# Half of the attention transposes moved from TensorE to VectorE, as nine 32x32 blocks a step, in a decoder kernel

## The chip, the core and the metric

The kernel runs on one core of a Trainium2 chip. A core has four engines that compute, each with its own instruction queue: TensorE (PE in the profile, with its weight loads as PEld), VectorE (DVE), ScalarE (ACT) and GpSimd (POOL); SyncE (SP) issues transfers. Semaphores order the queues against each other. The metric is the time of the whole kernel on the device in microseconds.

## What is computed

A decoder of four layers on x of 16 sequences x 128 positions x 256 channels. The change lies in layer 2, whose first part is grouped-query attention with 16 heads of 128 channels over 4 key/value heads, with a mask that leaves each query a window of 32 positions and the first 4:

```python
def _sink_window_mask(t):
    pos = jnp.arange(t)
    q = pos[:, None]
    k = pos[None, :]
    return (k <= q) & ((k < SINK) | (k >= q - WINDOW + 1))      # SINK 4, WINDOW 32

def _masked_softmax(scores, mask):
    floor = jnp.finfo(scores.dtype).min
    ms = jnp.where(mask, scores, floor)
    row_max = jnp.max(ms, axis=-1, keepdims=True)
    ...
    ex = jnp.exp(ms - row_max) * mask.astype(scores.dtype)
    denom = jnp.maximum(jnp.sum(ex, axis=-1, keepdims=True), 1e-09)
    return ex / denom
```

The other parts of layer 2 are a cross attention in which each query keeps its 54 largest scores, and a feed-forward part with activations and weights rounded to 8-bit levels. Each part ends with a residual sum and a layer norm.

## The kernel before

All ten parts of the decoder stand one after the other. Only layer 2 is touched: `layer2_all` (L2538) weaves its three parts into one software pipeline over the 16 sequences. `STEPS` is 23; step i (i from 0 to 22) does the self-attention of sequence i, the end of it and the start of the cross attention of i-1, the selection of i-2, the end of the cross attention of i-3, the rounding for the feed-forward part of i-4, the upper product and the inner rounding of i-5, the lower product of i-6 and the last norm of i-7. Each engine has its own `step(i)` (ScalarE L2776, VectorE L3022, TensorE L3231), a list of calls in a hand-written order. Each call waits for the semaphores that it needs and holds up what is queued behind it on its engine.

The self-attention of one sequence: queries and keys are projected (`project_kv`, `project_q` in four quarters q, L3077, copied out by `queries_out`), `scores` (L3089) puts 8 heads (a half h) into two PSUM banks, `shift` adds the mask and takes the row maxima on VectorE, `exps` runs on ScalarE, and `normalise` (L2867) divides on VectorE. For the product with the values the probabilities must stand with the keys on the partitions. So `turn_probs` (L3097) transposes the 8 heads of a half on TensorE, each a 128x128 f32 transpose, into the half's banks; `probs_moved` (L2686) copies them on ScalarE to `probsT`; `attend` (L3107) multiplies.

What stands around the change, in program order:

- VectorE, step i: copy of the values (L3027), `shift` for both halves, `largest(i-2)`, `normalise(i, 0)`, `scale_up(i-5)` (L2941), `select(i-2)` (L2898, ends with L2906 to L2910), `normalise(i, 1)` (L2870 to L2874), `add(i-1)` (L2876; L2878 is the residual sum, L2884 the variance), `scale_inner(i-5)` (ends with L2951), `freshen(i-1)`, `scale_x(i-4)` (ends with L2937), `scale_down(i-6)` (L2953; L2955 raises back_made), `add_x(i-3)`, `finish(i-7)`, and in the first 12 steps a piece of the rounding of the weights.
- TensorE, step i: both `scores`, `scores_x(i-2)`, `project_kv(i+1)`, `turn_probs_x(i-3)`, `up(i-5)`, `turn_inner(i-6)`, `output(i-1)`, `read_x(i-3)`, `project_q(i+1, 0)`, `down(i-6)`, `project_q(i+1, 1)`, `turn_probs(i, 0)`, `output_x(i-3)` (L3145; it waits for "added", the end of `add(i-1)`), `project_q(i+1, 2)` and `(i+1, 3)`, `turn_probs(i, 1)`, `turn_x(i-1)`, `turn_xq(i-4)`, `attend(i, 0)`, `queries_x(i-1)` (L3166), `attend(i, 1)`. `project_q(.., 3)` waits until `queries_out(.., 1)` has emptied the bank.
- ScalarE, second half of step i: `queries_out(i+1, 0)`, `root_x(i-1)` (L2726, waits for the variance of `add`), `root_n`, `root_f`, `queries_out(i+1, 1)`, `probs_moved(i, 0)`, `inner_rounded(i-5)` (L2756, waits for L2951), `queries_out(i+1, 2)`, `xq_rounded(i-4)` (L2738, waits for L2937), `queries_out(i+1, 3)`, `probs_moved(i, 1)`, `x_out(i-1)` (L2720), and so on.

`turn_probs(i, 1)` writes into banks 2 and 3. Bank 3 also holds the lower product of the feed-forward part, so from step 6 on it waits for "back_made" of `scale_down(i-6)`, which is on VectorE in the same step.

## Time and profile before

| | us |
|---|---|
| median of 3 runs | 2474.65 (2472.78 to 2476.43) |
| the profiled execution, and its span | 2477.81, 2476.0 |
| granted TensorE clock over the span, share of full | 0.928 |
| busy: TensorE, VectorE, ScalarE, GpSimd | 2114.1, 1859.2, 1482.2, 198.2 |
| layer 2 in the span | about 1521 to 2103 |

The profile gives for each instruction its line in the kernel, its start and duration, and, in square brackets, how long its engine idled before it and which instruction ended that wait. A matmul's weight load (LDWEIGHTS) is a record of its own on PEld and overlaps with the multiply before it; the starts of loads show the pace of TensorE's queue. Within a queue, records of neighbours overlap by some tens of nanoseconds. Step i of the layer is counted from VectorE's copy L3027: step 0 at 1525.32, step 9 at 1795.01.

### The profile page before, as it was taken

What the parts mean: (1) busy time and instruction counts of PE and PEld (TensorE: products, weight loads), DVE (VectorE), ACT (ScalarE), POOL (GpSimd) and SP (SyncE); (2) the same over time, 40 slices, a digit from 0 to 9 for tenths busy, and PEclk for the clock granted to TensorE, in tenths of its full rate; (3) what the DMA queues carried; (4) which work ended last, traced back from release to release, by engine and by line L of the source; (5) the groups of instructions that cost most, each with busy time, mean ns of one, the idle gap of its engine ahead of it and who ended that gap; (6) DMA issues with size and microseconds to landing.
All of it is one profiled execution on the core that took longest, in us unless ns stands there. A gap on an engine that the chain in (4) does not pass through costs nothing. (4 is left out here: it accounts for less than half of the span.)

```text
span 2476.0 us, 42560 instructions
## 1 busy us (share of the span) xinstructions
PE 2114.1 (85%) x17048; PEld 1606.8 (65%) x17048; DVE 1859.2 (75%) x3345; ACT 1482.2 (60%) x2484; POOL 198.2 (8%) x148
## 2 busy tenths in 40 slices
PE   7996458999999999999863798999999974888755
PEld 4665336777777787777751456888888862555633
DVE  4777666888998888898769525567887766678687
ACT  3654255777777767777546423667777765455346
POOL 0000100110100011010100240000000000100301
PEclk8999678999999999999986899999999996999977
DMA  3000012122222222222232464111010000200001
GB/s 155 2 2 12 13 55 73 52 65 54 66 54 61 71 80 63 55 66 55 60 112 94 146 150 152 59 22 45 27 33 5 6 16 1 79 1 1 15 1 34
DMA packets 162482, 130.96 MB, mean 53 GB/s; under 512 B 118256, under 2 KB 145520, under 8 KB 155632
## 3 DMA queue, kind: packets, MB, share of 16 engines
q1 hardware_dynamic: 158448, 121.83, 16.1%
q0 software_dynamic: 3840, 6.43, 1.3%
q8 instruction: 136, 2.23, 0.4%
q14 instruction: 58, 0.48, 0.1%
HBM read 106.42 MB, written 21.79 MB: 52 GB/s over the span
## 5 line engine op out<-in xcount | busy, mean ns | idle before, releaser
L1587 DVE SCALAR_TENSOR_TENSOR ctx_chan<-l1a_raw,l1a_cw,ctx_chan 128x1024 f32<-128x1024 f32 x192 | 231.9, 1276 | 3.5 <-issue 3.5
L1195 PE MATMUL banks<-x_chan,l1a_wp 128*128 128x512 f32 x512 | 224.4, 596 | 3.6 <-ACT l1a_vt L1483 3.6
L1195 PEld LDWEIGHTS banks<-x_chan,l1a_wp 128*128 128x128 f32 x512 | 97.6, 191 | 121.0 <-issue 116.3
L3086 PE MATMUL banks<-x_chan,more_weights_ahead 128*128 128x128 f32 x1024 | 121.9, 276 | 1.2 <-ACT l2a_kT L2670 1.2
L3086 PEld LDWEIGHTS banks<-x_chan,more_weights_ahead 128*128 128x128 f32 x1024 | 118.6, 192 | 4.3 <-ACT l2a_kT L2670 2.0
L1232 PE MATMUL banks<-l1a_wo,l1a_oT 128*128 128x256 f32 x512 | 118.4, 385 | 0.0
L3122 PE MATMUL banks<-l2a_wo,l2a_oT 128*128 128x256 f32 x512 | 114.3, 381 | 0.0
L1203 PE MATMUL banks<-l1a_wz,x_chan 128*128 128x256 f32 x512 | 114.1, 381 | 0.0
L1182 POOL TENSOR_TENSOR l1a_al<-l1a_aT,l1a_outer 128x1024 f32<-128x1024 f32 x32 | 74.9, 2362 | 481.3 <-DVE l1a_aT L1647 481.3
L1232 PEld LDWEIGHTS banks<-l1a_wo,l1a_oT 128*128 128x128 f32 x512 | 97.0, 192 | 13.8
L3122 PEld LDWEIGHTS banks<-l2a_wo,l2a_oT 128*128 128x128 f32 x512 | 96.2, 190 | 14.7 <-issue 1.5
L1203 PEld LDWEIGHTS banks<-l1a_wz,x_chan 128*128 128x128 f32 x512 | 97.0, 192 | 13.1 <-issue 0.5
L2683 ACT ACTIVATE l2a_masked<-l2a_masked,l2a_rowmax 128x128 f32<-128x128 f32 x256 | 98.9, 392 | 8.1 <-DVE l2a_rowmax L2865 6.5
L1431 ACT ACTIVATE l1a_raw<-banks 128x1024 f32<-128x1024 f32 x64 | 65.5, 1023 | 48.1 <-PE banks L1195 48.1
L2678 ACT ACTIVATE l2a_qT<-banks 128x512 f32<-128x512 f32 x64 | 37.9, 594 | 66.6 <-PE banks L3086 66.6
L123 PE MATMUL banks<-ident,x_tok 128*128 128x128 f32 x224 | 42.9, 356 | 40.7 <-ACT x_tok L191 18.0
L3644 ACT ACTIVATE l3a_probsT<-banks 128x512 f32<-128x512 f32 x64 | 38.1, 596 | 59.3 <-PE banks L3810 59.3
L1461 ACT ACTIVATE l1a_oT<-l1a_go 128x1024 f32<-128x1024 f32 x32 | 33.9, 1058 | 66.2 <-DVE l1a_go L1712 66.2
L1642 DVE TENSOR_TENSOR_SCAN l1a_e<-ctx_tok 128x1024 f32<-128x1024 f32 x32 | 71.4, 2273 | 1.1 <-DMA ctx_tok<-l1a_rows_mem 1.1
L1772 DVE TENSOR_TENSOR l1a_vt<-banks,l1a_vt 64x512 f32<-64x512 f32 x64 | 44.4, 694 | 36.1 <-PE banks L1260 36.0
L1433 ACT ACTIVATE ctx_chan<-banks,l1a_cw 128x1024 f32<-128x1024 f32 x64 | 71.0, 1109 | 0.0
L3027 DVE COPY l2a_vals<-l2a_ready 128x512 f32<-128x512 f32 x16 | 6.8, 427 | 81.9 <-PE banks L3112 72.0
(648 smaller groups left out, 5706.8 us busy)
## 6 DMA issues: line engine op xcount, KB each, us to landing
l1a_sq<-l1a_norm_mem SPq DMA_DIRECT2D x16, 1024.0 KB, 4.7
ctx_tok<-l1a_rows_mem SPq DMA_DIRECT2D x16, 1024.0 KB, 8.0
ctx_chan<-in_ctxT_dram SPq DMA_DIRECT2D x3, 2048.0 KB, 18.1
l1f_wgu<-in_l1f_wgu_dram SPq DMA_DIRECT2D x4, 1408.0 KB, 11.5
moe_sums<-l1x_zero SPq DMA_DIRECT2D x2, 2176.0 KB, 16.4
l1a_wp<-in_l1a_wp_dram SPq DMA_DIRECT2D x8, 512.0 KB, 5.7
l1f_wgu<-moe_sums SPq DMA_DIRECT2D x8, 512.0 KB, 7.4
x_chan<-in_xT_dram SPq DMA_DIRECT2D x4, 512.0 KB, 5.5
```

The source lines that it names most:

```text
L1182: P.tensor_tensor(heads(al, h), heads(aT, h), bc(outer[:], 1, HALF), ALU.mult).then_inc(s["al_made"], 1)
L1195: mm = MM(projected(i, u)[:, q * 512:(q + 1) * 512], wp[:, c, u * 128:(u + 1) * 128], g.xT[:, c, t0:t0 + 512], start=c == 0, stop=c == 1)
L1203: mm = MM(unit(2 + h)[:, b * 256:(b + 1) * 256], g.xT[:, c, t0:t0 + S], wz[:, c, :], start=c == 0, stop=c == 1)
L1232: mm = MM(unit(h)[:, b * 256:(b + 1) * 256], oT[:, HALF * h + 2 * b + r, :], wo[:, r, :], start=r == 0, stop=r == 1)
L1431: A(raw[:, u, :, CONV - 1:], now, ACT.Copy)
L1433: A(conv[:, u, :], projected(i, u), ACT.Copy, scale=cw[:, c, CONV - 1:]).then_inc(s["tap"], 1)
L1587: V.scalar_tensor_tensor(t, raw[:, u, :, j:j + S], cw[:, c, j:j + 1], t, ALU.mult, ALU.add).then_inc(s["conv_done" if step == 2 else "conv ...
L1642: V.tensor_tensor_scan(heads(e, h).rearrange("p k n -> p (k n)"), rows[:, h * 1024:(h + 1) * 1024], floor, 0.0, ALU.add, ALU.max).then_inc ...
L1772: V.tensor_tensor(highs(vt, q), quarter(q)[64:128], highs(vt, q), ALU.add).then_inc(s["vr_made"], 1)
L2683: ins = A(probs[:, k, :], masked[:, k, :], ACT.Exp, bias=rowmax[:, k:k + 1], scale=128 ** -0.5, accum_out=rsum[:, k:k + 1])
L3086: mm = mm_(ps[:, 4 + q % 2, k * 128:(k + 1) * 128], wq[:, c, SHARE * q + k, :], g.xT[:, c, tile(i)], start=c == 0, stop=c == 1)
L3122: mm = mm_(ps[:, 6, 0:D], oT[:, h, :], wo[:, h, :], start=h == 0, stop=h == HEADS - 1)
```

## The change

Half 0 of the heads is no longer transposed on TensorE. The new `turn_first` on VectorE transposes it in 32x32 blocks, from `probs` straight to `probsT`. Of the 16 blocks of a head only nine can hold anything but zero under the mask; the list `WINDOWED` names them as (block of queries, block of keys), and the others are set to zero once by a memset at the start. Each of the nine instructions takes its block for all 8 heads of the half: 32 partitions, 8 x 32 elements each. `turn_first(i)` stands on VectorE between `select(i-2)` and `normalise(i, 1)`. TensorE's `turn_probs(i, 0)` and ScalarE's `probs_moved(i, 0)` are gone, and `attend(i, 0)` waits for the new semaphore. The remaining `turn_probs(i)` keeps its place behind `project_q(i+1, 3)` and now has both waits on the banks.

```diff
@@ layer2_all
+        WINDOWED = ((0, 0), (1, 0), (1, 1), (2, 0), (2, 1), (2, 2), (3, 0), (3, 2), (3, 3))
...
-            def probs_moved(i, h):
-                act.wait_ge(s["probs_turned"], i * 2 + (h + 1))
-                A(heads(probsT, h), half_banks(h), ACT.Copy).then_inc(s["probs_out"], 1)
+            def probs_moved(i):
+                act.wait_ge(s["probs_turned"], i + 1)
+                A(heads(probsT, 1), half_banks(1), ACT.Copy).then_inc(s["probs_out"], 1)
@@ step(i), ScalarE
                 if more:
                     queries_out(i + 1, 1)
-                if now:
-                    probs_moved(i, 0)
                 if on(i - 5):
                     inner_rounded(i - 5)
...
                 if now:
-                    probs_moved(i, 1)
+                    probs_moved(i)
@@ VectorE
+            def turn_first(i):
+                v.wait_ge(s["normed"], i * 2 + 1)
+                for a, b in WINDOWED:
+                    queries, keys = slice(32 * a, 32 * a + 32), slice(32 * b, 32 * b + 32)
+                    ins = V.transpose(heads(probsT, 0)[keys, :, queries], heads(probs, 0)[queries, :, keys])
+                ins.then_inc(s["first_turned"], 1)
@@ step(i), VectorE
                 if on(i - 2):
                     select(i - 2)
                 if i < B:
+                    turn_first(i)
                     normalise(i, 1)
...
+            V.memset(heads(probsT, 0), 0.0).then_inc(s["cleared"], 1)
             v.wait_ge(s["loaded"], 16)
+            v.wait_ge(s["cleared"], 1)
@@ TensorE
-            def turn_probs(i, h):
-                pe.wait_ge(s["normed"], i * 2 + (h + 1))
-                if h == 0 and i >= 5:
+            def turn_probs(i):
+                pe.wait_ge(s["normed"], i * 2 + 2)
+                if i >= 5:
                     pe.wait_ge(s["gu_done"], i - 4)
-                if h == 1 and i >= 6:
+                if i >= 6:
                     pe.wait_ge(s["back_made"], i - 5)
                 for k in range(HALF_HEADS):
-                    mm = turn(half_banks(h)[:, k, :], heads(probs, h)[:, k, :], g.ident[:])
+                    mm = turn(half_banks(1)[:, k, :], heads(probs, 1)[:, k, :], g.ident[:])
                 mm.then_inc(s["probs_turned"], 1)
             def attend(i, h):
                 pe.wait_ge(s["vals_moved"], i + 1)
-                pe.wait_ge(s["probs_out"], i * 2 + (h + 1))
+                pe.wait_ge(s["probs_out" if h else "first_turned"], i + 1)
@@ step(i), TensorE
                 if more:
                     project_q(i + 1, 1)
-                if now:
-                    turn_probs(i, 0)
                 if on(i - 3):
                     output_x(i - 3)
                 if more:
                     project_q(i + 1, 2)
                     project_q(i + 1, 3)
                 if now:
-                    turn_probs(i, 1)
+                    turn_probs(i)
```

## Rows read from the trace of the kernel before

**Rows 1.** Steps 6 to 13: stretch, length; busy us of PE, PEld, DVE, ACT, POOL; clock, DMA.

```profile
1698.28:1956.23 257.95, 257.95 (x1722) 217.76 (x1721) 201.95 (x531) 192.09 (x512) 4.29 (x8) 1.00 0.08 23
```

**Rows 2.** Timeline of VectorE in step 9: start, us, engine, line, instruction, [idle before].

```profile
1810.80 0.29 DVE L2910 TENSOR_SCALAR l2a_px<-l2a_px,l2a_sumx 128x128 f32<-128x128 f32 x1
1811.00 0.16 DVE L2870 TENSOR_SCALAR l2a_rsum<-l2a_rsum 128x8 f32<-128x8 f32 x1
...
1812.58 0.42 DVE L2878 TENSOR_TENSOR x_tok<-banks,x_tok 128x256 f32<-128x256 f32 x1
...
1818.14 0.48 DVE L2955 SCALAR_TENSOR_TENSOR ctx_tok<-banks,l2a_sh,l2f_row 128x256 f32<-128x256 f32 x1
...
1827.25 0.43 DVE L3027 COPY l2a_vals<-l2a_ready 128x512 f32<-128x512 f32 x1 [3.00 <-PE banks L3112]
```

**Rows 3.** Timeline of TensorE's weight loads in step 9.

```profile
1816.05 0.91 PEld L3104 LDWEIGHTS banks<-ident,l2a_masked 128*128 128x128 f32 x8
1816.92 0.73 PEld L3153 LDWEIGHTS banks<-l2a_wox,l2a_ox 128*128 128x128 f32 x4
...
1821.36 0.91 PEld L3104 LDWEIGHTS banks<-ident,l2a_masked 128*128 128x128 f32 x8
```

**Rows 4.** Groups by line and shape in layer 2: count, busy us, mean ns, idle before.

```profile
L3027 DVE COPY l2a_vals<-l2a_ready 128x512 f32<-128x512 f32 x16 | 6.8, 427 | 81.9 <-PE banks L3112 72.0 <-ACT l2a_ready L2674 9.9
L2688 ACT ACTIVATE l2a_probsT<-banks 128x1024 f32<-128x1024 f32 x32 | 32.7, 1023 | 10.1 <-PE banks L3104 10.0
```

**Rows 5.** Timeline of VectorE at the end of the kernel, instructions without waits between.

```profile
2468.98 0.74 DVE L144 BATCH_NORM_STATS2 ln_stats_buf<-x_tok 128x6 f32<-128x256 f32 x2
...
2470.69 1.38 DVE L3531 TENSOR_SCALAR x_tok<-x_tok,ln_moments_buf,ln_rstd_buf 128x256 f32<-128x256 f32 x4
```

**Rows 6.** Timeline of VectorE and of the weight loads, step 0.

```profile
1544.51 0.17 DVE L2870 TENSOR_SCALAR l2a_rsum<-l2a_rsum 128x8 f32<-128x8 f32 x1 [2.37 <-ACT l2a_masked L2683]
...
1544.95 1.23 DVE L2874 TENSOR_TENSOR l2a_masked<-l2a_masked,l2a_rsum 128x1024 f32<-128x1024 f32 x1
...
1548.99 0.91 PEld L3104 LDWEIGHTS banks<-ident,l2a_masked 128*128 128x128 f32 x8
```

**Rows 7.** Timeline of ScalarE and of the weight loads, step 2.

```profile
1598.32 0.20 ACT L2728 ACTIVATE ln_rstd_buf<-ln_rstd_buf 128x1 f32<-128x1 f32 x1 [0.48 <-DVE ln_rstd_buf L2884]
...
1599.03 0.60 ACT L2678 ACTIVATE l2a_qT<-banks 128x512 f32<-128x512 f32 x1 [0.51 <-PE banks L3086]
...
1599.59 3.65 PEld L3086 LDWEIGHTS banks<-x_chan,more_weights_ahead 128*128 128x128 f32 x32
```

**Rows 8.** Timeline of VectorE and of the weight loads, step 3.

```profile
1624.88 0.42 DVE L2878 TENSOR_TENSOR x_tok<-banks,x_tok 128x256 f32<-128x256 f32 x1
...
1628.02 0.73 PEld L3153 LDWEIGHTS banks<-l2a_wox,l2a_ox 128*128 128x128 f32 x4
```

**Rows 9.** Timeline of VectorE, the weight loads and ScalarE, step 5.

```profile
1685.21 0.42 DVE L2878 TENSOR_TENSOR x_tok<-banks,x_tok 128x256 f32<-128x256 f32 x1
...
1687.95 0.73 PEld L3153 LDWEIGHTS banks<-l2a_wox,l2a_ox 128*128 128x128 f32 x4
...
1688.44 0.16 DVE L2951 RECIPROCAL l2a_rh<-l2a_sh 128x1 f32<-128x1 f32 x1
...
1689.18 0.96 ACT L2758 ACTIVATE ctx_tok<-ctx_tok,l2a_toround,l2a_rh 128x704 f32<-128x704 f32 x1
...
1693.57 1.02 ACT L2688 ACTIVATE l2a_probsT<-banks 128x1024 f32<-128x1024 f32 x1 [0.28 <-PE banks L3104]
```

**Rows 10.** Timeline of VectorE and of the weight loads, step 6.

```profile
1721.64 0.48 DVE L2955 SCALAR_TENSOR_TENSOR ctx_tok<-banks,l2a_sh,l2f_row 128x256 f32<-128x256 f32 x1
...
1724.63 0.91 PEld L3104 LDWEIGHTS banks<-ident,l2a_masked 128*128 128x128 f32 x8
```

**Rows 11.** Timeline of VectorE and of the weight loads, step 15.

```profile
2011.60 0.48 DVE L2955 SCALAR_TENSOR_TENSOR ctx_tok<-banks,l2a_sh,l2f_row 128x256 f32<-128x256 f32 x1
...
2012.19 1.57 PEld L3104 LDWEIGHTS banks<-ident,l2a_masked 128*128 128x128 f32 x8 [4.89 <-issue]
```

More of the change, by code:

```diff
@@ L2584, in layer2_all @@
         s = L.sem_set("loaded w_loaded next_loaded wox_loaded staged queries keys values q_out k_out v_out vals_moved scores maxed "
-                      "masked lowered exped rs normed probs_turned probs_out pv o_out out added "
+                      "masked lowered exped rs normed cleared first_turned probs_turned probs_out pv o_out out added "
                       "wr_loaded w_summed w_floored w_scaled w_spread wt_loaded w_rows w_divided w_rounded w_quantised "
```

## The prediction

> **What bounds the kernel now.** I read the windows of the layer first. In the eight steps 6 to 13 TensorE is busy for 257.95 of 257.95 us at full clock, VectorE for 201.95 and ScalarE for 192.09 [rows 1]. So TensorE sets the step of 32.24 us, in which VectorE works 25.2 and ScalarE 24.0, and the step repeats itself up to step 14. Next I read VectorE's own order in step 9: it idles 3.0 us at the seam of two steps, waiting for the last attention product (L3112), then works with almost no gap [rows 2]. So on a busy-time account this change takes work from the full engine and gives it to one that has room. The views that decide are others: where in the step the added work stands, and how long before its use TensorE gets what VectorE makes behind that place. I measure such a lead as TensorE's weight load (it starts the group) minus the end of the VectorE instruction it waits for, minus the 0.11 us from such an end to the load: in step 15, where the load did wait, 2012.19 against 2011.60 + 0.48 [rows 11].
>
> In step 9 the two leads are:
> - output_x (L3153) waits for add (L2878): 1816.92 against 1812.58 + 0.42 + 0.11 = 1813.11, lead 3.81 us [rows 2, 3].
> - the second turn_probs (L3104) waits for scale_down (L2955, "back_made"): 1821.36 against 1818.14 + 0.48 + 0.11 = 1818.73, lead 2.63 us [rows 2, 3]. This is the tighter one, and it exists only from step 6 on. Steps 7 to 14 show the same pair at the same distances.
>
> **What goes.** The eight TensorE transposes of half 0: the loads of L3104 start at 1816.05 and those of L3153 behind them at 1816.92, so the group takes 0.87 us of TensorE's queue [rows 3]. That is the whole possible gain: 16 x 0.87 = 13.9 us. The copy of half 0 out of the banks (L2688, 1.02 us, one of two a step) leaves ScalarE [rows 4], which idles 8 us a step; by itself that gains nothing. attend(i, 0) waits for the block transposes instead; in step 9 they are done at about 1814.2, and it stands behind the second turn_probs, at 1821.36 or later.
>
> **What comes.** Nine VectorE instructions a step, each on 32 partitions with 8 x 32 = 256 elements per partition, in a row without waits between them. The trace has no block transpose and no 32-partition instruction. The nearest rows are f32 instructions of 256 elements per partition. Alone one takes 0.42 us [rows 2]. Back to back they overlap: four take 1.38 us, (1.38 - 0.42) / 3 = 0.32 us from start to start; two take 0.74 [rows 5]. I bound the nine from 9 x 0.32 = 2.9 us (full overlap) to 9 x 0.42 = 3.8 us (none) and take 9 x 0.345 = **3.1 us**, near the lower end, since instructions that do not wait for each other show the overlap. Call it T.
>
> The page "VectorE: DVE Perf Modes" of the Trainium skill (section on the three transpose paths) gives 311 ns for a VectorE transpose of 128x128 bf16. The 128-element TENSOR_SCALAR just ahead of the new place takes 0.29 us [rows 2]. An estimate from the page: 0.02 us more each than a plain instruction, T = 3.1 to 3.2, the sum at most 1.4 us higher.
>
> The memset of 1024 elements costs at most about a plain instruction of that size, 1.2 us [rows 6], and stands in the 9.9 us that VectorE idles before its first copy [rows 4]: nothing. If that cover were gone it would be 1.2 us once.
>
> **Where T falls.** It stands between select (ends with L2910) and normalise(i, 1) (starts with L2870). In step 9 L2910 ends at 1811.09 and L2870 starts at 1811.00 [rows 2]: there is no idle to fill, and none up to L2955. Everything behind comes T later: normalise 1, add, scale_inner, freshen, scale_x, scale_down. The 3 us of idle lie at the seam, behind all of them, so they can't shield them. Now step by step, with the change of each step's length:
>
> - Steps 0 and 1: no select yet. VectorE idles 2.37 us for the exponentials just where T stands, so only 3.1 - 2.37 = 0.7 us come through; normalise ends at 1544.95 + 1.23 = 1546.18, its use is at 1548.99 [rows 6]. TensorE keeps its gain: -0.87 each, **-1.7**.
> - Step 2: select is there, T comes through whole. ScalarE's root_x (L2728, at 1598.32) waits for add's variance, and queries_out(1), 0.60 us, stands behind it. root_x moves to 1601.42, queries_out(1) starts 0.1 us before its 0.20 are over, at 1601.52, and ends 1602.12; project_q(3), which needs it, starts near 1602.2. It started in the middle of the 3.65 us of loads from 1599.59, at 1601.38 [rows 7]. **+0.85**, that is T - 2.25.
> - Steps 3 and 4: output_x waits for add. 1625.30 + 0.11 + 3.1 = 1628.51 against 1628.02 [rows 8]: **+0.5** each, T - 2.6.
> - Step 5: add ends at 1685.63; + 0.11 + 3.1 = 1688.84 against 1687.95: +0.9. Here inner_rounded is on ScalarE for the first time. It starts at 1689.18 and waits for VectorE's L2951, which moves to 1688.60 + 3.1 = 1691.7 [rows 9]. Behind it stand queries_out(2), xq_rounded and queries_out(3), with it an estimated 3.2 us, so probs_moved starts near 1694.9, where TensorE's shift of 0.9 alone would bring it to 1694.5. x_out, and with it queries_x, is late by the difference. **+1.4**.
> - Step 6: scale_down ends at 1722.12, the load starts at 1724.63 [rows 10]: lead 2.40, **+0.7**.
> - Steps 7 to 14: output_x may start at 1813.11 + 3.1 = 1816.21, 0.71 us early. project_q(2) and (3) follow, and turn_probs could load at 1820.65, but scale_down lets it only at 1818.73 + 3.1 = 1821.83, against 1821.36 before. The gain is gone in a wait of 1.2 us: 8 x (3.1 - 2.63) = **+3.8**. ScalarE reached probs_moved 9.3 us after add's old end in step 5; here that is 1822.3, and the transposes come out only at about 1823.0, so it adds nothing.
> - Step 15: no projections are left, and TensorE already waits 4.89 us (loads) at turn_probs for L2955 [rows 11]. T goes in whole: **+3.1**. The transposes behind that wait run at the lower clock (eight loads in 1.57 us against 0.91) [rows 3, 11]; they do so already, so I add nothing.
> - Steps 16 to 22 have no transposes.
>
> Sum: -1.7 + 0.85 + 1.0 + 1.4 + 0.7 + 3.8 + 3.1 = **+9.2 us**. The profiled execution took 2477.81 us (span 2476.0), 3.2 above the median of 2474.65; the difference is put on the median: 2483.8. About 14 us per us of T: with T = 2.9 the sum is +6.4, with 3.8 it is +19.0.
>
> The next thing that would be late, were back_made's wait not there, is VectorE's own round: of 3.0 us at the seam 3.0 - 2.63 = 0.4 stay, whatever T is, because TensorE is pushed back with it.
>
> **Rivals.**
> - *The blocks are cheap, and the kernel is faster.* The plain copy of 512 elements takes 0.43 us [rows 4], half the time per element. If the transposes ran at that rate, 256 elements would take 0.29 us alone, 0.20 from start to start, T = 1.8. Then -1.7 in steps 0 and 1, -0.45 in 2, -1.6 in 3 and 4, -0.4 in 5, -0.6 in 6, 8 x -0.83 = -6.6, +1.8 in 15: **-9.6 us, 2465**. From T = 3.1 - 9.2 / 14 = 2.44 down the kernel is faster. Against it: the 256-element instructions of rows 5 don't show it. The page "Vector Engine (DVE) Microarchitecture Reference" (3.8) says the transposing front-end sustains one element per cycle per lane; that is a rule against this rival, and no row here tests it.
> - *Nothing measurable.* If T is 2.5 to 2.75 (a 32-partition instruction with a shorter start), or one lead is longer than it looks because the waits order themselves anew, the 0.87 and the wait balance: **+1 to +4 us, 2478**. For it: the gap between gain and loss is only 0.5 us a step. Against it: no pair of rows 5 is closer than 0.32 us.
> - *The blocks are dear.* Four-byte elements could take twice the cycles, or each block be one instruction with its own start. Nine at about 0.6 us (0.27 more than 0.33) are T = 5.4: 9.2 + 14 x 2.3 = **+41 us, 2516**. For it: nothing in the trace excludes it. Against it: f32 costs no more per element than that in any row here.
> - *The gain holds.* VectorE would have to take T out of its idle time. It can't: the idle is behind the instructions that TensorE waits for [rows 2]. It is part of the first rival's chance.
>
> **How the numbers follow.** Forecast (T 2.9 to 3.8, +6.4 to +19.0, so 2481 to 2494) 0.64; dear 0.14; nothing measurable 0.13; cheap 0.09. The predicted time is 2484. The range of 2477 to 2497 holds the forecast and most of the rival beside it, and the lower edge of the dear one, about 0.8. A measurement of this kernel can tell about 0.2%, 5 us, from no change. Slower by more than that: nearly all of the forecast and the dear case, 0.76; within it: the case of nothing measurable and a little of its neighbours, 0.14; faster: the cheap case and a T just above it, 0.10.
>
> **What would show it.** In the profile after: nine transposes a step with 0.32 to 0.42 us from start to start between L2910 and L2870; a step from 7 to 14 of 32.24 + (T - 2.63) = 32.7 us; TensorE with a wait of about 1.2 us at turn_probs, ended by VectorE's scale_down, and one of some 0.2 us before output_x; VectorE's idle at the seam down from 3.0 to about 0.4; in step 15 a wait of over 7 us. Steps 0 and 1 should be shorter by 0.9. A step under 32.24 us would make the forecast wrong through T; a wait that ends on something other than scale_down would make it wrong in its mechanism.

## The result and the profile after

The changed kernel takes **2497.60 us** (median of 4 runs, 2492.26 to 2500.84) against 2473.74 for the kernel before (4 runs, 2472.78 to 2476.43): ratio 1.0092, 95% interval 1.0075 to 1.0109. It is slower by 23.9 us; 9.2 were forecast, and the time lies 0.6 us above the upper end of the range. The profiled execution took 2498.36 us (span 2496.6, clock 0.928). TensorE's busy time fell from 2114.1 to 2098.9 us, ScalarE's from 1482.2 to 1465.8, VectorE's rose from 1859.2 to 1923.0. Everything that was to be unloaded is unloaded, and the kernel is slower.

The line numbers shift: L3033 is the copy of the values (L3027 before), L2884 the residual sum of `add` (L2878), L2961 the instruction of "back_made" (L2955), L3113 `turn_probs` (L3104), L3162 `output_x` (L3153), L2879 the new block transposes.

First the windows of steps 6 to 13, which answer [rows 1] (columns as there), then the group of the new instructions (count, busy us, mean ns, idle before):

```profile
1701.74:1970.90 269.16, 254.01 (x1651) 211.67 (x1658) 233.41 (x603) 183.98 (x504) 4.29 (x8) 1.00 0.07 22
```

```profile
L2879 DVE STREAM_TRANSPOSE l2a_probsT<-l2a_masked 32x256 f32<-32x256 f32 x144 | 62.6, 435 | 1.8
```

Eight steps take 269.16 us, 33.64 each, where they took 257.95. TensorE was busy all of that time before; now it has 15 us of gaps. Neither queue is full: VectorE works 233.4 of 269.2 us. So the step is set by waits that run back and forth between the two. The timeline of VectorE in step 9 answers [rows 2] (start, us, engine, line, instruction):

```profile
1802.67 0.43 DVE L3033 COPY l2a_vals<-l2a_ready 128x512 f32<-128x512 f32 x1 [0.52 <-PE banks L3121]
...
1818.46 0.29 DVE L2916 TENSOR_SCALAR l2a_px<-l2a_px,l2a_sumx 128x128 f32<-128x128 f32 x1
1818.66 4.02 DVE L2879 STREAM_TRANSPOSE l2a_probsT<-l2a_masked 32x256 f32<-32x256 f32 x9
1822.71 0.17 DVE L2869 TENSOR_SCALAR l2a_rsum<-l2a_rsum 128x8 f32<-128x8 f32 x1
...
1824.30 0.42 DVE L2884 TENSOR_TENSOR x_tok<-banks,x_tok 128x256 f32<-128x256 f32 x1
...
1829.87 0.48 DVE L2961 SCALAR_TENSOR_TENSOR ctx_tok<-banks,l2a_sh,l2f_row 128x256 f32<-128x256 f32 x1
```

The nine take 4.02 us (4.02 or 4.03 in every step; T is 4.03 below), and the next instruction starts 4.05 us after their start. One lasts 0.435 us (the group's mean above). From start to start that is (4.02 - 0.435) / 8 = 0.448 us, more than one lasts: they do not overlap at all. Everything behind them is late by about T. Seen from the copy, L2884 starts at 21.63 us, where it was 17.57, and L2961 at 27.20, where it was 23.13; the idle before the next copy (the seam of two steps) fell from 3.00 to 0.31 us. Whom that hits stands in TensorE's own timeline of the same step, which answers [rows 3]:

```profile
1824.87 1.10 PE L3162 MATMUL banks<-l2a_wox,l2a_ox 128*128 128x256 f32 x4 [0.89 <-DVE x_tok L2884]
...
1830.50 1.06 PE L3113 MATMUL banks<-ident,l2a_masked 128*128 128x128 f32 x8 [0.96 <-DVE ctx_tok L2961]
```

Both waits of the prediction are there, ended by the two instructions that it named. PE's idle counts from the modelled end of the matmul before, so it comes out shorter than the delay. The prediction measured by the starts of the weight loads, and these give the delay:

```profile
1824.84 0.73 PEld L3162 LDWEIGHTS banks<-l2a_wox,l2a_ox 128*128 128x128 f32 x4 [1.05 <-issue]
1825.59 3.76 PEld L3095 LDWEIGHTS banks<-x_chan,more_weights_ahead 128*128 128x128 f32 x32
1830.47 0.85 PEld L3113 LDWEIGHTS banks<-ident,l2a_masked 128*128 128x128 f32 x8 [1.12 <-issue]
```

The loads of output_x start 22.17 us after the copy; in the kernel without the blocks (below), where nothing waits, they start at 21.04. That is a delay of 1.13 us. The transposes start 4.88 us behind the loads of `project_q` (1830.47 - 1825.59), without a wait 3.67: a delay of 1.21 us. Together they are 2.34 us, near 0.87 + 1.40, the gain used up and the growth of the step.

Three places at the beginning and the end of the pipeline follow. Step 5: the timelines of TensorE and of ScalarE, then the windows of TensorE's wait and of the work behind it (columns as in [rows 1]; the third number from the end is the granted clock):

```profile
1689.80 1.75 PE L3162 MATMUL banks<-l2a_wox,l2a_ox 128*128 128x256 f32 x4 [2.49 <-DVE x_tok L2884]
```

```profile
1692.66 0.97 ACT L2759 ACTIVATE ctx_tok<-ctx_tok,l2a_toround,l2a_rh 128x704 f32<-128x704 f32 x1 [1.33 <-DVE l2a_rh L2957]
```

```profile
1687.30:1689.70 2.40, 0.01 (x1) 0.00 (x0) 2.27 (x6) 0.00 (x0) 0.00 (x0) 1.00 0.00 0
1689.80:1692.00 2.20, 2.20 (x8) 1.89 (x9) 2.10 (x5) 0.78 (x3) 0.00 (x0) 0.57 0.00 0
1692.00:1695.80 3.80, 3.80 (x29) 3.80 (x29) 3.45 (x14) 2.73 (x4) 0.00 (x0) 0.80 0.00 0
```

After 2.49 us without work TensorE's granted clock, full until then, is 0.57 and 0.80 in the two stretches behind: it was at the lower of its two levels, 1.2 GHz, for part of them. The 32 loads of `project_q` take 5.01 us there instead of the 3.76 of step 9. Behind the waits of 2.35 us in step 2 and 2.09 us in step 3 the clock stayed at 1.00. And step 15, which answers [rows 11]:

```profile
2026.68 2.04 PE L3162 MATMUL banks<-l2a_wox,l2a_ox 128*128 128x256 f32 x4 [6.42 <-DVE x_tok L2884]
...
2032.30 1.94 PE L3113 MATMUL banks<-ident,l2a_masked 128*128 128x128 f32 x8 [3.58 <-DVE ctx_tok L2961]
```

**Where the 23.9 us come from.** The steps are taken from one copy of the values to the next, the changed kernel's minus those of the kernel before. Steps 0 and 1: -0.57 and -0.87 us. Step 2: +1.75. Steps 3 and 4: +1.46 and +1.44. Step 5: +3.49. Step 6: +1.41. Steps 7 to 14: 8 x 1.40 = +11.2. Together +19.3. In step 15 L2961 starts 27.18 us after the copy against 23.13, +4.05, and from the copy of step 15 to the first matmul of the next layer the profile after takes 4.3 us more, this delay included. That makes 23.6 us, the measured difference within its interval. In this one profile layer 2 also began 3.27 us earlier than in that of before, though nothing ahead of it was changed, so the two profiled executions differ by 20.55 us only.

### The profile page after: what moved, and what is told of

It is laid out like the page before. It is cut to its first block and busy times, and to the rows that moved or that the text cites. A ratio compares the mean times of both kernels' runs of the same rounds, so it can differ in the third digit from the quotient of the medians.

```text
span 2496.6 us, 42374 instructions
## 1 busy us (share of the span) xinstructions
PE 2098.9 (84%) x16871; PEld 1593.0 (64%) x16920; DVE 1923.0 (77%) x3490; ACT 1465.8 (59%) x2468; POOL 196.4 (8%) x148
## 5 line engine op out<-in xcount | busy, mean ns | idle before, releaser
L123 PEld LDWEIGHTS banks<-ident,x_tok 128*128 128x128 f32 x224 | 34.9, 188 | 48.3 <-ACT x_tok L191 19.6
L1260 PE MATMUL banks<-l1a_uw,l1a_al 64*64 64x128 f32 x512 | 65.2, 280 | 0.0
```

The source lines that it names most:

```text
L123: mm = nc.tensor.transpose(g.ps[:, n % 2, t * 128:(t + 1) * 128], g.x[:, t0 + t, c * 128:(c + 1) * 128], g.ident[:])
```

## Experiments

Ratios are against the kernel before, run on the same chip at the same time; the brackets hold the 95% interval. T is the time that the added instructions take on VectorE, read from the trace. Where blocks are left out or replaced, that half of the heads comes out wrong; such a kernel is for its time alone.

### How much of the loss hangs on T: none, four, six of the nine

```diff
-                    turn_first(i)
...
-                pe.wait_ge(s["probs_out" if h else "first_turned"], i + 1)
+                if h:
+                    pe.wait_ge(s["probs_out"], i + 1)
+                else:
+                    pe.wait_ge(s["normed"], 2 * i + 1)
```

> The changed kernel without its nine block transposes: half 0 of the heads is transposed by nobody, so the attention output of those heads is left out of what is computed rightly; all else stands as in the changed kernel. Theory A (only the time T that the transposes put ahead of add and scale_down on VectorE costs; TensorE's 0.87 us a step is a real gain while nothing is late): T = 0, all leads hold, 15 steps shorter by 0.87 us, 13 us less than the kernel before, ratio 0.9947; steps 7 to 14 take 31.37 us. Theory B (another wait takes over once TensorE is shorter, ScalarE's order or a bank wait, and part of the 24 us lost is that): less than 6 us gained, steps near 32 us, with a TensorE wait that ends on ScalarE.

```diff
-                for a, b in WINDOWED:
+                for a, b in WINDOWED[:4]:
```

> The changed kernel with the first four of the nine blocks only; the other five are left out. Theory A: from the trace after, a transpose costs 0.448 us from start to start, T = 1.8 us. That is under both leads even with TensorE 0.87 us ahead (2.63 - 0.87 = 1.76 at turn_probs, to 0.03 us), so steps 7 to 14 take 31.4 us; step 2 gains 0.5, steps 3 and 4 0.8 each, step 15 loses 1.8. Sum about -10 us against the kernel before, ratio 0.996. Theory B (a cost of mixing the transposes in at all, a switch of VectorE's mode or a port, beside their own durations): no better than the kernel before.

With `WINDOWED[:6]`:

> The changed kernel with the first six of the nine blocks; the other three are left out. Theory A (the step pays for what T exceeds the lead of 2.63 us by): 6 x 0.448 = 2.7 us, steps 7 to 14 take 32.24 + 0.05 = 32.3 us, the step of the kernel before. Steps 0 and 1 gain 1.7, step 15 loses 2.7, steps 2 to 6 lose about 1.4 in all. Sum +3 us, ratio 1.001 (0.999 to 1.003). Theory B (the loss grows with VectorE's busy time from the first block on, without a threshold): two thirds of the changed kernel's +24, or 4 blocks' -5 plus 0.4 of the way: +6 to +16, ratio 1.0025 to 1.0065.

Measured: none 0.9960 (0.9944 to 0.9975), steps of 31.37 us; four 0.9978 (0.9967 to 0.9989), steps of 31.38; six 1.0011 (1.0001 to 1.0021), steps of 32.27. The steps are as expected in all three. The whole of none and of four gained less than their expectations (0.9947 and 0.996; the latter lies outside the interval); the table at the end of this part says where that went. The window 1740 to 1960 of none, the group of the four and, of the six, the transposes and the wait that they cause in step 9:

```profile
1740.00:1960.00 220.00, 219.63 (x1448) 184.84 (x1454) 176.70 (x466) 162.14 (x442) 3.76 (x7) 1.00 0.05 16
```

```profile
1803.72 1.77 DVE L2879 STREAM_TRANSPOSE l2a_probsT<-l2a_masked 32x256 f32<-32x256 f32 x4
```

```profile
1807.34 2.66 DVE L2879 STREAM_TRANSPOSE l2a_probsT<-l2a_masked 32x256 f32<-32x256 f32 x6
```

```profile
1817.80 1.06 PE L3113 MATMUL banks<-ident,l2a_masked 128*128 128x128 f32 x8 [0.71 <-DVE ctx_tok L2961]
```

Without the blocks TensorE is full again, and its step is 32.24 - 0.87 = 31.37: in the steps the gain of the prediction is real and of its size. With four, six and nine blocks the step is 29.61 us + T: 31.38 at 1.77, 32.27 at 2.66, 33.64 at 4.03. TensorE's own 31.37 is the floor, reached at T = 1.76, and at T = 2.63 the step equals the 32.24 of before. That is the lead that the prediction read from [rows 2, 3] and put against T; 0.87 of it pays for TensorE's gain.

### The transposes added to the kernel before, nothing taken away

```diff
@@ step(i), VectorE, kernel before
                 if i < B:
+                    turn_first(i)
                     normalise(i, 1)
```

> The kernel before, complete, and the nine block transposes beside it at the same place of VectorE, into the same tile; TensorE's transposes and ScalarE's copy stay and overwrite it (the copy waits for the blocks too, which are done 2 us earlier). Theory A: what TensorE saves is worth nothing from step 2 on, because VectorE's scale_down and add set it; steps 6 to 14 take 33.64 us as in the changed kernel, steps 0 and 1 stay as before; 1 to 3 us slower than the changed kernel, some 26 us over the kernel before, ratio 1.010 to 1.011. Theory B (part of the loss comes from taking work out of TensorE's and ScalarE's order): clearly faster than the changed kernel. Theory C (TensorE's time adds up with the wait): slower than the changed kernel by 0.87 x 14 = 12 us, ratio 1.015.

Measured: 1.0109 (1.0090 to 1.0129), steps 7 to 14 of 33.62 to 33.65 us. TensorE in step 9:

```profile
1828.10 1.06 PE L3115 MATMUL banks<-ident,l2a_masked 128*128 128x128 f32 x8 [0.95 <-DVE ctx_tok L2965]
```

The step is the same 33.64 us whether TensorE and ScalarE keep their share or not. With the share kept, the wait before output_x is gone (TensorE arrives 0.87 us later) and the one of 0.95 us at turn_probs remains. So the loss is VectorE's addition alone, and what TensorE saves in these steps is spent in waiting. Theory C, that TensorE's time adds up with the wait, falls. The early steps add a control for the clock: in step 5 TensorE waits 1.61 us there, the clock stays at 1.00, the 32 loads take 3.76 us, and the step grows by 2.17 us (30.64 to 32.81) instead of 3.49.

### The same nine, behind the instruction that TensorE waits for

```diff
-                    turn_first(i)
                     normalise(i, 1)
...
@@ scale_down(j), behind the instruction of back_made
+                if j + 6 < B:
+                    turn_first(j + 6)
@@ step(i), VectorE
                 if on(i - 6):
                     scale_down(i - 6)
+                elif i < B:
+                    turn_first(i)
```

> The changed kernel, complete, with all nine block transposes moved on VectorE from between select and normalise to just behind the first instruction of scale_down (in steps 0 to 5: behind scale_x). Theory A: VectorE does the same work, but only attend(i, 0) waits for it. In steps 7 to 14 they end at 23.61 + 4.03 + 0.11 = 27.75 us into the step, attend loaded at 27.61 before: +0.14 us a step. Steps 1 to 4 gain 0.8 to 0.9 each, step 0 loses 0.5, step 5 1.4, step 6 0.4, step 15 1.7. Sum about +2 us against the kernel before, ratio 1.0006 (0.998 to 1.003), some 22 us faster than the changed kernel. Theory B (VectorE as a whole is too full with 64 us more work): as slow as the changed kernel, ratio 1.009.

Measured: 1.0005 (0.9992 to 1.0019), steps 6 to 14 of 31.7 to 32.6 us. Step 9, VectorE and TensorE:

```profile
1812.40 4.02 DVE L2879 STREAM_TRANSPOSE l2a_probsT<-l2a_masked 32x256 f32<-32x256 f32 x9
```

```profile
1816.56 1.96 PE L3124 MATMUL banks<-l2a_probsT,l2a_vals 128*128 128x512 f32 x4 [0.76 <-DVE l2a_probsT L2879]
```

The same 4.02 us on the same engine, and the loss is gone: it came from the place of the work, not from its amount. Now `attend(i, 0)` waits for them, for 0.76 us, so the gain is not there either.

### Why the nine take 4.02 us

First the block transposes replaced by plain copies of the same slices, at the same place:

```diff
-                    ins = V.transpose(heads(probsT, 0)[keys, :, queries], heads(probs, 0)[queries, :, keys])
+                    ins = V.tensor_copy(heads(probsT, 0)[keys, :, queries], heads(probs, 0)[queries, :, keys])
```

> The changed kernel with nine plain copies of the same 32-partition, 8 x 32 element slices in place of the nine transposes, across the same quarters of the partitions; the blocks land unturned, so the output of those heads is not what is to be computed. It asks what makes a transpose cost 0.448 us from start to start. Theory C (it is the transposing itself: plain instructions overlap and copies move two f32 a cycle): 0.20 us from start to start, T = 1.8, steps 7 to 14 take 31.4 us, ratio 0.996 to 0.998 as with four blocks. Theory D (32-partition slices or the way across quarters cost it): about 0.45, T = 4.0, ratio 1.009.

```profile
L2879 DVE COPY l2a_probsT<-l2a_masked 32x256 f32<-32x256 f32 x144 | 40.9, 284 | 1.8
```

```profile
1808.85 2.66 DVE L2879 COPY l2a_probsT<-l2a_masked 32x256 f32<-32x256 f32 x9
```

Ratio 1.0012 (1.0002 to 1.0022), steps of 32.27 us, just as with six transposes of the same 2.66 us: only T counts. But from start to start the copies are (2.66 - 0.284) / 8 = 0.297 us apart, where neither theory had them: shorter than transposes, yet again without any overlap. So it is not the transposing that forbids it. Then groups of four on VectorE ahead of the layer's first step, all but one of them reading partitions 0 to 31 (a quarter below is one of the four groups of 32 partitions):

```diff
+            top, here, there = slice(0, 32), slice(0, 32), slice(32, 64)
+            zero, aside = heads(probsT, 0), heads(probs, 1)
+            for k in range(4):
+                ins = V.transpose(aside[here, :, 32 * k:32 * k + 32], zero[top, :, 0:32])
+            ins.then_inc(s["probe"], 1)
+            v.wait_ge(s["probe"], 1)
...
+            for k in range(4):
+                ins = V.tensor_copy(aside[here, :, 32 * k:32 * k + 32], zero[top, :, 0:32])
```

> The changed kernel, complete, with eight groups of four VectorE instructions ahead of the layer's first step, on zeroed data that nothing reads: transposes of 32 x 256 within a quarter, across quarters, of 32 x 128, of 32 x 32, of 128 x 128, and 32 x 256 as a copy, a TENSOR_SCALAR and a TENSOR_TENSOR. It measures starts, not the kernel's time. Theory C: transposes of 256 elements 0.45 us from start to start in both directions, 128 elements 0.31, 32 elements 0.21: a fixed part of about 0.18 with no overlap, and one element a cycle behind it; the 128 x 128 one also 0.31, since partitions work in parallel; the copy 0.20, the other two 0.32. Theory D: within a quarter clearly less than across; plain 32-partition instructions at 0.4 or more. Theory E (f32 blocks take two cycles an element and the fixed part is nothing): 0.45, 0.23 and 0.06.

```profile
1514.44 1.41 DVE L3071 STREAM_TRANSPOSE l2a_masked<-l2a_probsT 32x256 f32<-32x256 f32 x4
1515.89 1.41 DVE L3075 STREAM_TRANSPOSE l2a_masked<-l2a_probsT 32x256 f32<-32x256 f32 x4
...
1518.76 0.89 DVE L3087 STREAM_TRANSPOSE l2a_masked<-l2a_probsT 128x128 f32<-128x128 f32 x4
1519.68 0.89 DVE L3091 COPY l2a_masked<-l2a_probsT 32x256 f32<-32x256 f32 x4
1520.61 0.89 DVE L3095 TENSOR_SCALAR l2a_masked<-l2a_probsT 32x256 f32<-32x256 f32 x4
1521.53 1.42 DVE L3099 TENSOR_TENSOR l2a_masked<-l2a_probsT 32x256 f32<-32x256 f32 x4
...
1534.37 4.03 DVE L2879 STREAM_TRANSPOSE l2a_probsT<-l2a_masked 32x256 f32<-32x256 f32 x9
```

Here they do overlap: (1.41 - 0.42) / 3 = 0.33 us apart for the transposes, (0.89 - 0.284) / 3 = 0.20 for the copies, and in the same trace the layer's nine again take 4.03. The second group writes another quarter of the partitions than it reads, and that costs nothing. None of the three theories had this: C and E put 0.45 us on these transposes, D a difference between the first two groups. What differs from the layer's nine is that no quarter changes from one instruction to the next. That was tried by itself:

```diff
+            quarter = lambda k: slice(32 * k, 32 * k + 32)
+            for k in range(4):
+                ins = V.transpose(aside[quarter(0), :, 32 * k:32 * k + 32], zero[quarter(0), :, 0:32])
...
+                ins = V.transpose(aside[quarter(k), :, 32 * k:32 * k + 32], zero[quarter(0), :, 0:32])
...
+                ins = V.transpose(aside[quarter(0), :, 32 * k:32 * k + 32], zero[quarter(k), :, 0:32])
...
+                ins = V.transpose(aside[quarter(k), :, 32 * k:32 * k + 32], zero[quarter(k), :, 0:32])
```

> The changed kernel with six groups of four VectorE instructions ahead of the layer's first step, each instruction 32 partitions x 256 elements in f32, with a semaphore wait between the groups. Four groups of block transposes: (1) all reading and writing quarter 0 of the partitions; (2) all reading quarter 0, writing quarters 0, 1, 2, 3; (3) reading quarters 0, 1, 2, 3, all writing quarter 0; (4) both changing. Two groups of copies: (5) as 2, (6) as 3. The question is what keeps the layer's nine from overlapping: start to start they take 0.448 us, where the first probe's four in one quarter took 0.33. Theory H (a VectorE instruction whose first partition for its input or its output differs from that of the instruction before it starts only when that one is done): group 1 takes 1.41 us as in the first probe, groups 2, 3 and 4 each 3 x 0.448 + 0.42 = 1.76 to 1.78 us, groups 5 and 6 3 x 0.297 + 0.28 = 1.17 us. Theory I (only a change of the input's quarter matters): group 2 at 1.41 and group 5 at 0.89, groups 3, 4 and 6 as in H. Theory J (only a change of the output's quarter matters): the reverse. Theory K (the quarters have nothing to do with it, but the data or the waiting engines of the layer): all four groups of transposes 1.41 us, both groups of copies 0.89 us. The time of the whole kernel is of no interest.

In the order of the groups: none changes, output changes, input changes, both; copies with the output changing, with the input changing.

```profile
1517.87 1.41 DVE L3071 STREAM_TRANSPOSE l2a_masked<-l2a_probsT 32x256 f32<-32x256 f32 x4
1519.31 1.78 DVE L3075 STREAM_TRANSPOSE l2a_masked<-l2a_probsT 32x256 f32<-32x256 f32 x4
1521.13 1.77 DVE L3079 STREAM_TRANSPOSE l2a_masked<-l2a_probsT 32x256 f32<-32x256 f32 x4
1522.93 1.78 DVE L3083 STREAM_TRANSPOSE l2a_masked<-l2a_probsT 32x256 f32<-32x256 f32 x4
1524.75 1.18 DVE L3087 COPY l2a_masked<-l2a_probsT 32x256 f32<-32x256 f32 x4
1525.96 1.17 DVE L3091 COPY l2a_masked<-l2a_probsT 32x256 f32<-32x256 f32 x4
```

Theory H holds in all six. Here an instruction whose first partition, of input or of output, lies in another quarter than that of the instruction before it starts only when that one is done. Either change is enough, and both together cost no more. And in the layer, with nine of which only two change quarter:

```diff
-                for a, b in WINDOWED:
-                    queries, keys = slice(32 * a, 32 * a + 32), slice(32 * b, 32 * b + 32)
-                    ins = V.transpose(heads(probsT, 0)[keys, :, queries], heads(probs, 0)[queries, :, keys])
+                for a, b in ((0, 0), (0, 1), (0, 2), (0, 3), (1, 0), (1, 1), (1, 2), (1, 3), (2, 0)):
+                    rows, cols = slice(32 * a, 32 * a + 32), slice(32 * b, 32 * b + 32)
+                    ins = V.transpose(heads(probsT, 0)[rows, :, cols], heads(probs, 0)[rows, :, cols])
```

> The changed kernel with its nine block transposes at the same place, of the same shape and with the same waits, but four of them read and write quarter 0, the next four quarter 1 and the last one quarter 2 (so the transposed values of this half of the heads are other ones and the output is not the reference's). The first partition changes twice between the nine and not eight times. Theory H (a change of quarter forbids the overlap): from start to start six times 0.33 and twice 0.448, then one duration of 0.435, together 3.31 us for the nine where the changed kernel took 4.02. With the steps at 29.61 us plus the time of the nine, as in the changed kernel (33.64 at 4.03) and in the ones with six blocks and with copies (32.27 at 2.66), steps 7 to 14 come to 32.9 us, PE waits about 1.4 us per step for turn_probs (0.72 with six blocks, twice that with the rest at output_x), and the ratio to the kernel before is about 1.005 (between 1.0012 at 2.66 us and 1.0092 at 4.03). Theory K (the layer's work around them slows them): the nine stay at 4.0 us, steps 33.64 us, ratio 1.009.

```profile
1813.80 3.28 DVE L2879 STREAM_TRANSPOSE l2a_probsT<-l2a_masked 32x256 f32<-32x256 f32 x9
```

```profile
1824.88 1.06 PE L3113 MATMUL banks<-ident,l2a_masked 128*128 128x128 f32 x8 [0.95 <-DVE ctx_tok L2961]
```

3.28 us (3.31 expected), steps of 32.90, ratio 1.0044 (1.0030 to 1.0058). The wait at turn_probs is 0.95 us, the one before output_x 0.15 where the profile shows it: 1.1 together where 1.4 was expected. By the starts of the loads in step 9 the delays are 0.38 and 1.20 us, together 1.58, against T - 1.76 = 1.52: what falls short is PE's modelled idle, not the delay. The real nine can't be sorted like this: each is its own pair of a block of queries (input) and a block of keys (output), so between any two of them at least one changes, and one is enough.

The Trainium skill has the rule, as a model, page "VectorE: DVE Perf Modes", section "Two Vector instructions with no wait between them": an instruction whose start quadrant (a group of 32 partitions) differs from that of the last read or write is held until all earlier ones have finished. These runs agree with it, with 0.448 against 0.33 us for the transposes and 0.297 against 0.20 for the copies. The same page's section "The DRAIN you can't avoid" says at first that no instruction starts before the pipe is empty, and then makes an exception of those that are not held; the groups at 0.33 and 0.20 us are that exception.

### An order that keeps the gain

The cost of T depends on what stands behind it. In this complete kernel `normalise(i, 1)` and `add` come first, then one block, `freshen`, `scale_x`, the first instruction of `scale_down`, and there the other eight; `scale_inner` goes last, and ScalarE's `inner_rounded`, which waits for it, to the end of its step.

```diff
@@ step(i), ScalarE
-                if on(i - 5):
+                if i >= B and on(i - 5):
                     inner_rounded(i - 5)
...
                 if now:
                     attended(i, 1)
+                if i < B and on(i - 5):
+                    inner_rounded(i - 5)
@@ VectorE
-            def turn_first(i):
+            def turn_first(i, early=False):
...
-                for a, b in WINDOWED:
+                for a, b in WINDOWED[:1] if early else WINDOWED[1:]:
...
-                ins.then_inc(s["first_turned"], 1)
+                if not early:
+                    ins.then_inc(s["first_turned"], 1)
@@ scale_down(j), behind the instruction of back_made
+                if j + 6 < B:
+                    turn_first(j + 6)
@@ step(i), VectorE
                 if i < B:
-                    turn_first(i)
                     normalise(i, 1)
...
-                if on(i - 5):
+                if i < B:
+                    turn_first(i, early=True)
+                elif on(i - 5):
                     scale_inner(i - 5)
...
                 if on(i - 6):
                     scale_down(i - 6)
+                elif i < B:
+                    turn_first(i)
+                if i < B and on(i - 5):
+                    scale_inner(i - 5)
```

> A complete kernel meant to beat both: the nine block transposes stay on VectorE, but in order of deadlines. In steps 0 to 15 VectorE does normalise 1, add, one block (while it waits for ScalarE's root), freshen, scale_x, the first instruction of scale_down, the other eight blocks, and only then scale_inner; ScalarE's inner_rounded goes to the end of the step, since its result is used in the next one. Theory A: no TensorE wait ends late any more; steps 12 to 14 take 31.4 us. In steps 6 to 11, where VectorE also rounds weights, its own round binds (the four-block kernel had 0.32 + 1.36 us of idle a step, 2.2 us of blocks more use it up): 31.9 to 32.0. Steps 1 to 5 gain 0.87 each. Sum -8 us against the kernel before, ratio 0.9967 (0.994 to 0.9995). Theory B (VectorE with 64 us more work is too full for any order): no better than the kernel before, ratio 1.000 to 1.005.

```profile
1740.00:1960.00 220.00, 219.63 (x1448) 184.85 (x1454) 203.00 (x529) 161.93 (x442) 4.17 (x8) 1.00 0.06 16
```

```profile
1807.26 0.48 DVE L2964 SCALAR_TENSOR_TENSOR ctx_tok<-banks,l2a_sh,l2f_row 128x256 f32<-128x256 f32 x1
1807.77 3.58 DVE L2881 STREAM_TRANSPOSE l2a_probsT<-l2a_masked 32x256 f32<-32x256 f32 x8
```

Ratio 0.9970 (0.9958 to 0.9982), 2469.17 against 2475.98 us: 0.3% faster than the kernel before, though its eight take 3.58 us, 0.448 each. TensorE is as busy as with no blocks at all, 219.63 of 220 us. Steps 6 to 14 take 282.3 us together, against 9 x 32.24 = 290.2. Is this the order alone? The kernel before with the same new order and without the blocks:

```diff
@@ step(i), ScalarE, kernel before
-                if on(i - 5):
+                if i >= B and on(i - 5):
                     inner_rounded(i - 5)
...
                 if now:
                     attended(i, 1)
+                if i < B and on(i - 5):
+                    inner_rounded(i - 5)
@@ step(i), VectorE
-                if on(i - 5):
+                if i >= B and on(i - 5):
                     scale_inner(i - 5)
...
                 if on(i - 6):
                     scale_down(i - 6)
+                if i < B and on(i - 5):
+                    scale_inner(i - 5)
```

> The kernel before with the order of work of the complete reordered kernel and without the block transposes: scale_inner last in VectorE's step, inner_rounded at the end of ScalarE's, both up to step 15, all transposes on TensorE. The question is whether the reordered kernel (0.997, steps of 31.4 to 31.6 us) gains by the TensorE time that the change frees, or by the new order alone. Theory A (the gain is TensorE's: in steps 7 to 14 TensorE has no idle time in the kernel before, steps 32.24 us, and an order of the other engines can't shorten them): steps 7 to 14 stay at 32.24, the ratio is 1.000, at best 0.999, and at worst 1.002 if the later int8 rows make TensorE wait. Theory M (the new order alone brings the gain): steps of 31.4 us or less in 7 to 14, ratio 0.997.

```profile
1740.00:1960.00 220.00, 220.00 (x1477) 185.93 (x1476) 171.61 (x450) 163.26 (x427) 3.76 (x7) 1.00 0.05 16
```

Ratio 1.0019 (1.0005 to 1.0034), steps of 32.24 us with no gap on TensorE. The order alone gains nothing: its steps are those of before. The gain of the reordered kernel is the 0.87 us a step that the moved transposes free on TensorE (its steps 6 to 14 are 31.37 us in the mean).

**All runs in one table.** Differences to the kernel before in us: steps 0 to 14, then the layer in the profile (from the first copy of the values to the first matmul of the next layer), then the whole, from the ratio.

| run | T | steps 0 to 14 | layer | whole |
|---|---|---|---|---|
| changed kernel | 4.03 | +19.3 | +23.6 | +23.9 |
| e_both | 4.03 | +18.8 | +23.7 | +27.0 |
| e_same | 3.28 | +7.6 | +12.8 | +10.9 |
| e_6blocks | 2.66 | +0.1 | +2.9 | +2.7 |
| e_copies | 2.66 | -0.5 | +2.7 | +3.0 |
| e_4blocks | 1.77 | -11.3 | -7.5 | -5.4 |
| e_none | 0 | -12.7 | -10.7 | -9.9 |
| e_late | 4.03, later | -1.5 | +0.9 | +1.2 |
| e_order | 4.03, split | -11.3 | -7.2 | -7.4 |
| e_orderonly | 0 | -0.3 | +2.5 | +4.7 |

Every layer difference lies within the interval of its whole. What the steps do not hold comes behind the copy of step 15. For T > 0 part of it is T itself, but e_none and e_orderonly add nothing to VectorE and are 1.9 and 2.7 us longer there. In their profiles 1.9 and 1.8 us of that fall between the residual sum of `add` in step 16 and that of `add_x` in step 17, where TensorE's granted clock was lower than in the profile before. The first 14 us of this stretch, before and in e_orderonly:

```profile
2031.38:2045.38 14.00, 7.94 (x46) 6.26 (x44) 8.39 (x27) 7.92 (x17) 0.00 (x0) 0.88 0.00 0
```

```profile
2027.75:2041.75 14.00, 8.65 (x43) 6.98 (x42) 8.39 (x27) 7.24 (x15) 0.00 (x0) 0.72 0.00 0
```

The changed kernel's profile has 0.88 there too, e_none 0.73. Why the clock differs is not shown.

## Why the prediction came out as it did

**What bounds the kernel, and which waits decide: right.** The leads of 2.63 and 3.81 us, read from two timelines, carried over: steps 7 to 14 grew by T - 2.63 = 1.40 us, steps 3 and 4 by T - 2.6 = 1.4 to 1.5, step 2 by T - 2.25 = 1.8 (1.75), and output_x was late by 1.13 us where the lead of 3.81 less the gain of 0.87 gives T - 2.94 = 1.09. TensorE waits for `add` and for "back_made" as named; e_both and e_late exclude the other causes, TensorE's altered order and a full VectorE.

**The size of T: wrong, and this is the step that failed.** The prediction bounded the nine from 2.9 to 3.8 us, with the upper end as "9 x 0.42 = 3.8 us (none)" of overlap, and took 3.1 near the lower, "since instructions that do not wait for each other show the overlap". The rows for it [rows 5] were all instructions over 128 partitions, one like the other, so no quarter ever changed in them. The nine change at every one and take 9 x 0.448 = 4.03 us. The term that failed is the overlap; e_probe, e_probe2 and e_same show what removes it. The upper end was short too: one 32x256 transpose lasts 0.435 us and the next starts 0.013 later, against the 0.42 taken from another instruction. The slope of "about 14 us per us of T" makes 0.93 x 14 = 13 us of that, so 9.2 becomes 22.2.

**Term by term at T = 4.03** (formula of the prediction, then measured): steps 0 and 1 -1.7, -1.4; step 2 +1.8, +1.75; steps 3 and 4 +2.9, +2.9; step 5 +2.3, +3.49; step 6 +1.6, +1.41; steps 7 to 14 +11.2, +11.2; step 15 +4.0, +4.05, and +0.25 behind it. Sum +22.1 against +23.6. Most of the rest, 1.2 us, is step 5.

**Step 5: mis-sized by the clock.** The estimate of ScalarE's chain from inner_rounded to probs_moved, 3.2 us, was right at full clock: in e_both it is 3.15. In the changed kernel TensorE's wait before output_x grew to 2.49 us, its granted clock fell, and `project_q` took 1.25 us more. The two runs that hold the changed kernel's steps behind a probe show the same 32 loads at 5.03 and 5.21 us. The prediction looked for the lower clock in step 15 alone. The length of the wait is not all that decides. In step 2 TensorE waits 2.35 us in the changed kernel and in both runs with a probe. Here is the stretch behind that wait, in the changed kernel and in e_probe2 (the third number from the end is the granted clock):

```profile
1599.80:1603.00 3.20, 3.20 (x21) 2.39 (x20) 0.29 (x1) 1.90 (x3) 0.00 (x0) 1.00 0.60 178
```

```profile
1599.80:1603.10 3.30, 3.30 (x19) 3.30 (x18) 0.40 (x1) 0.82 (x2) 0.00 (x0) 0.52 0.60 193
```

The clock stayed full in the changed kernel (and in e_probe) and fell in e_probe2, whose step 2 grew by 3.40 us instead of 1.75. What else decides stays open; in the changed kernel step 2 might as well have cost those 1.65 us more.

**The rivals.** "Nothing measurable" needed a T of 2.5 to 2.75; e_6blocks and e_copies show what it would have brought at 2.66: ratios of 1.0011 and 1.0012, +2.7 and +3.0 us, as it said. "Cheap" was worked out at T = 1.8 as -9.6 us; e_4blocks, at 1.77, measured -5.4. "Dear" put a block at 0.6 us; the measured 0.448 lies between it and the forecast's 0.345, nearer the forecast. Of its two reasons the first, more cycles for four-byte elements, is not what happened: one of the nine lasts 0.435 us, a TENSOR_TENSOR of 256 elements 0.42, and only the overlap is missing. The second, that each block would have its own start, came near: the nine start one after the other, at 0.448 us. The estimate from the Trainium skill's 311 ns (page "VectorE: DVE Perf Modes") put a surplus into the transposing, 0.02 us for each. In the groups without a change of quarter there is none (four transposes take 1.41 us, four TENSOR_TENSOR 1.42), so that it went the right way is luck; and nine times 0.02 on 3.1 is 3.3, not at most 3.2. "The gain holds" falls at this place and holds at another (e_order), by the order of the work and not by idle time that was there before.

**What was to be seen.** The seam's idle of about 0.4 us was 0.31 in step 9. The delay of 1.2 us at turn_probs was 1.21 by the starts of the loads. The one before output_x was 1.13 rather than 0.2: once output_x waits at all, what T grows by is added there, and the delay at turn_probs stays the same (1.20 in e_same, at T = 3.28). In step 15 the wait of over 7 us did not come at turn_probs. TensorE waits 6.42 us before output_x and 3.58 at turn_probs, 10.0 together, against 1.34 + 4.52 = 5.9 in the profile before; the growth is T.

## To carry to other kernels

Price work that is moved to another engine by the lead of what stands behind its new place, not by that engine's busy time. Here the first 1.76 us were free in steps 7 to 14, the next 0.87 used up the gain, and behind 2.63 each further 0.1 us cost about 1.4 us over the kernel; the same work a few instructions later left the time where it was before the change. Before taking an overlap from rows of neighbouring instructions, see whether they share their first partition. Where the quarter changes each time, count the full duration plus 0.013 us for each, as measured here for transposes and copies. A wait that grows on TensorE may cost more than its length: look at the granted clock behind it.

## What the runs showed of the hardware that was not expected

- In these groups VectorE overlapped neighbouring instructions only while their inputs and outputs started in the same quarter of the partitions as the last ones: 0.33 against 0.448 us from start to start (transposes, 32x256 f32), 0.20 against 0.297 (copies). Reading one quarter and writing another costs nothing as long as both stay.
- A block transpose of f32 is no dearer than a TENSOR_TENSOR on as many elements: four of 32x256 take 1.41 us, four TENSOR_TENSOR 1.42, but four copies and four TENSOR_SCALAR 0.89. By the elements per partition it is the same on all partitions: four of 128x128 take 0.89 us, and four of 32x128 took 0.88 in the same trace.
- In three profiles of the same steps (after, e_probe, e_probe2) the granted clock stayed full behind TensorE's waits of 2.09 us (steps 3 and 4) and fell behind the one of 2.49 us (step 5); behind the one of 2.35 us (step 2) it stayed full twice and fell once.
